# A four-layer attention kernel: the last layer's head moves one iteration ahead, and its exponentials are added up on VectorE alone

## The chip, the cores and the metric

The kernel runs on one core of a Trainium2 chip. The metric is the device time of one execution in microseconds (us); the median of three runs is given. The engines are TensorE (PE, its weight loads are PEld), VectorE (DVE), ScalarE (ACT), GpSimd (POOL) and SyncE (SP, which here only issues DMAs). Each works through its own instructions in order and waits on semaphores.

## The reference

Eight batches of 256 channels x 1024 positions go through four layers. Cut to what matters:

```
x: (8, 256, 32, 32)
L0: q, k, v of 32 channels, softmax attention over 1024 positions, projected and added to x;
    then attention from 1024 positions to 128 concepts, projected and added
L1: q, k of 32 channels, v of 256, softmax attention, x + gamma * out
L2: group norm, q, k, v of 256 channels, one head, softmax attention, projection, x + out
L3: group norm, q, k, v of 256 channels in 8 heads of 32:
    scores = q @ k.T / sqrt(sqrt(32)) ; probs = softmax(scores) ; ctx = probs @ v
    out = layer_norm(ctx @ wo.T + bo) + x
```

All is in float32; the scores are built from high and low parts, so that they keep their precision.

## The kernel before

A batch goes through two halves. Its *front* is layers 0 to 2, its *back* is layer 3, the last layer. `batches` (L150) runs them in three parts: first the fronts of batches 0 and 1 side by side ("fronts"), then six iterations, each with the front of batch b + 2 beside the back of batch b ("both"), then the backs of batches 6 and 7 side by side ("backs"). Every half is written as a generator that issues the instructions of one engine and yields after each slot; `merged` (L136) interleaves two generators of one engine by a fixed table, `ORDER` (L75): numbers of slots, in turn from the second and from the first of the two. So the order on each engine is written out, and an instruction that waits holds all behind it on its engine.

The back of a batch, in order:
- *head*: group norm 3 (DVE statistics, two tiny PE matmuls, ACT log and exponential, DVE and ACT write `hb`); queries and keys of the first four heads (four `project` calls, L605, 16 matmuls as the trace counts them), high parts on ACT (L1067), low parts on DVE (L1280); the values of all heads (L616, 32 matmuls) into `vb`; then SP copies high and low parts into stacks with 24 DMAs (`stacks`, L466)
- *round 0* (`u` = 0, four heads): 32 maxima (PE `max_tile`, L621, two matmuls of 512 columns each into two banks; DVE reduces them, L1285), DVE's transpose and four DMAs that bring the maxima into a row of the queries; queries and keys of the other four heads; 16 steps (`steps`), each with four score matmuls (L641), four exponentials (ACT, L1138), and one weighing of the values (L918)
- *round 1*: the same for the other four heads, without a projection
- the output projection, layer norm (L1498, L1502) and the store.

The sum of the exponentials over the keys is made by adding tiles. In each step from the second on in either half of the queries (14 of the 16 steps), DVE adds the first pair of heads (`add_weights`, L1436, the instruction at L1446), POOL the second pair (L555), each 128 x 1024. The exponentials of a step go into one of two buffers, so ACT waits for both additions before it writes a buffer again (L1131). At the end of a half PE sums over the partitions (L930), ACT makes the logarithm and its exponential, DVE multiplies (L1454).

The front's layers follow the same pattern with one head: `layer0`, `layer1`, `layer2` on PE; maxima (L1285), scores, exponentials (L1008), weighing (L755), POOL's additions (L523, L528), PE's sum (L762), normalising (L1334, L1338). The first matmuls of the front (L608 with `xm`) wait for the input, which SP loads into `xm[b % 3]` (L488) once DVE has read the residual of the back three batches earlier.

The back's tiles are `hb`, `part`, `qs`, `ks`, `vb`, `prb`, `accb`; the front of batch 1 uses the same memory, and the back of batch 7 uses the tiles of the fronts. The back of batch 0 waits on DVE for all of batch 1's front (L1425).

Of the kernel before, what the change touches and what calls it, by code (L numbers as in the profile page):

```python
# [22 lines left out]

# [9 lines left out]
B = 8  # L33
# [25 lines left out]
for _name, _n in (("gn_w2", 2), ("gn_b2", 2), ("bq2", 2), ("bk2", 2), ("bo2", 2), ("gn_w3", 2), ("gn_b3", 2),  # L59
# [36 lines left out]
    ("fronts", "ACT"): (  # L96
        0, 4, 4, 14, 1, 2, 1, 2, 1, 1, 9, 1, 3, 1, 5, 4, 5, 12, 2, 2, 4, 1, 2, 1, 1, 2, 1, 2, 2, 3, 8, 3, 2, 1,
        1, 7, 3, 1, 9, 4, 2, 2, 2, 2, 1, 2, 3, 1, 2, 2, 3, 1, 1, 3, 2, 2, 2, 1, 2, 3, 3,),
    ("both", "ACT"): (
        0, 2, 1, 1, 1, 1, 6, 21, 10, 3, 4, 1, 33, 1, 6, 1, 2, 1, 3, 2, 4, 1, 2, 1, 3, 1, 3, 1, 2, 5, 2, 21, 21,  # L100
        1, 6, 1, 2, 1, 8, 2, 2, 1, 6, 1, 8, 1, 4, 1, 2, 1, 4, 3, 4, 3, 2, 1, 5, 1, 1, 1, 4, 1, 3, 3,),
    ("backs", "ACT"): (
        0, 2, 1, 1, 2, 5, 5, 73, 2, 1, 72, 54, 6, 2, 2, 1, 1, 1, 1, 3, 3, 1, 4, 1, 1, 1, 1, 1, 2, 1, 5, 1, 6, 1,
        1, 4, 4, 2, 3, 1, 1, 1, 4, 1, 4, 2, 3, 1, 8, 1, 4, 1, 18,),
    ("fronts", "DVE"): (
        0, 4, 1, 2, 1, 2, 1, 2, 1, 2, 8, 8, 1, 1, 1, 1, 1, 2, 2, 4, 1, 1, 1, 1, 1, 2, 4, 3, 11, 11, 1, 1, 2, 5,
        1, 5, 6, 2, 3, 2, 2, 1, 4, 2, 2, 1, 2, 1, 6, 3, 1, 1, 1, 2, 1, 1, 6, 2, 1, 1, 1, 1, 2, 4, 4,),
    ("both", "DVE"): (
# [3 lines left out]
    ("backs", "DVE"): (  # L112
# [4 lines left out]
    ("fronts", "POOL"): (  # L117
        0, 5, 4, 3, 4, 1, 1, 3, 3, 2, 2, 1, 1, 1, 1,),
    ("both", "POOL"): (
        10, 1, 3, 1, 1, 6, 6, 1, 3, 1, 3, 2, 2, 4,),  # L120
    ("backs", "POOL"): (
        0, 14, 14, 11, 1, 1, 1, 1, 3, 1, 9,),
    ("fronts", "SP"): (
        0,),
    ("both", "SP"): (
        16,),
    ("backs", "SP"): (
        0, 6, 6, 7, 7, 1, 1, 2, 2,),
# [20 lines left out]

def batches(engine, front, back):  # L150

    finish(merged("fronts", engine, front(0), front(1)))
    for b in range(B - 2):
        finish(merged("both", engine, front(b + 2), back(b)))
    finish(merged("backs", engine, back(B - 2), back(B - 1)))
# [31 lines left out]
def attention_layers(nc, x, weights, vectors, small, concepts, constants, out):  # L187
    with ExitStack() as ctx:
# [255 lines left out]
        def _(sp):  # L444
# [9 lines left out]
            def program(o):  # L454
# [48 lines left out]
        def _(pool):  # L503
# [7 lines left out]
            def program(o):  # L511
# [31 lines left out]
                def back(b):  # L543
# [16 lines left out]
                    def nothing(u):  # L560
                        yield from ()
# [994 lines left out]
```

## Time and profile before

| | us |
|---|---|
| median of 3 runs | 3000.66 (2998.16 to 3001.39) |
| the profiled execution | 3000.55 |
| its span, first to last instruction | 2998.4 |
| busy: PE / DVE / ACT / POOL | 2740.4 / 1795.9 / 1209.4 / 897.0 |

The page gives for each engine the time in which it was busy, then the chain of work that ended last, and the costliest groups of instructions with their mean duration. The windows give the same busy times for a stretch between two points of time, with the granted clock of PE (1.00 is 2.4 GHz, 0.5 is 1.2 GHz). The timeline lists an engine's instructions with start, duration, and how long the engine was idle before and what ended that. A busy PE is not a PE at its peak: matmuls overlap, and at the lower clock the same work is busy for longer.

### The profile page before, as it was taken

The numbers are of one execution on the slowest core, as the hardware profiler recorded it, in microseconds if no ns is written. First come the engines' busy times: TensorE is split into PE (matmuls) and PEld (weight loads), VectorE is DVE, ScalarE is ACT, GpSimd is POOL, SyncE is SP. The second block draws the span as 40 slices with busy tenths as digits, with TensorE's granted clock in tenths as the row PEclk, the third lists the DMA queues.
The fourth block names the chain that finished last, engine by engine and source line by source line (L and its number), as shares of the span: only waits on it lengthen the run. The fifth ranks groups of instructions, "written<-read, shape, count | busy, mean of one in ns | idle before, by whom it ended". The sixth has DMA issues, their size and how long they took to land.

```text
span 2998.4 us, 25561 instructions
## 1 busy us (share of the span) xinstructions
PE 2740.4 (91%) x9636; PEld 1415.0 (47%) x9636; DVE 1795.9 (60%) x1749; ACT 1209.4 (40%) x2073; POOL 897.0 (30%) x362
## 2 busy tenths in 40 slices
PE   7999989999899998999889998999989989798887
PEld 4546644455444544445444454444544445443332
DVE  4535057673676647765476654767447583488884
ACT  3332223535344442534426254262532625325455
POOL 0040311614025240333304242061510615115563
PEclk8899988989788998989979898798987989879787
DMA  2000010100201002010010100101020100211100
GB/s 83 1 0 0 1 43 1 43 1 6 65 1 43 1 17 54 1 42 1 28 43 1 42 1 29 42 14 30 1 56 15 40 3 1 64 36 43 43 1 28
DMA packets 29291, 72.08 MB, mean 24 GB/s; under 512 B 10224, under 2 KB 10416, under 8 KB 28912
## 3 DMA queue, kind: packets, MB, share of 16 engines
q1 hardware_dynamic: 29168, 70.45, 9.4%
q8 instruction: 76, 1.25, 0.2%
q14 instruction: 47, 0.39, 0.0%
HBM read 11.40 MB, written 8.39 MB: 7 GB/s over the span
## 4 chain that ended last, share of the span: by engine, by line
PE 71%; DVE 17%; issue 3%; ACT 3%; SPq 2%; DMA 2%; POOL 1%; DVEq 0%; ACTq 0%; POOLq 0%
PE ps L755 13%; PE ps L608 12%; PE ps L641 9%; PE ps L627 9%; PE ps L918 7%; PE ps L840 6%; DVE ba_nmx L1285 5%; PE ps L616 4%; SPq L477 2%; PE ps L697 2%; DVE accb L1446 2%; PE ps L826 2%; DVE fa_nmx L1285 1%; PE ps L930 1%; PE ps L837 1%
## 5 line engine op out<-in xcount | busy, mean ns | idle before, releaser
L1138 ACT ACTIVATE prb<-ps 128x512 f32<-128x512 f32 x896 | 489.1, 598 | 367.7 <-PE ps L641 341.1
L1285 DVE TENSOR_REDUCE ba_nmx<-ps 128x1 f32<-128x1024 f32 x448 | 531.0, 1215 | 77.9 <-PE ps L627 76.2
L555 POOL TENSOR_TENSOR accb<-accb,prb 128x1024 f32<-128x1024 f32 x168 | 440.8, 2624 | 179.0 <-ACT prb L1138 174.8
L627 PE MATMUL ps<-ks,qs 96*128 96x512 f32 x896 | 419.5, 575 | 74.6 <-DVE ba_nmx L1285 69.0
L555 POOL TENSOR_TENSOR accb<-prb 128x1024 f32<-128x1024 f32 x28 | 80.2, 2864 | 1306.8 <-ACT prb L1138 1247.3
L755 PE MATMUL ps<-pr,h 128*128 128x512 f32 x896 | 421.1, 594 | 0.2
L1446 DVE TENSOR_TENSOR accb<-accb,prb 128x1024 f32<-128x1024 f32 x168 | 317.8, 1892 | 155.8 <-ACT prb L1138 154.1
L641 PE MATMUL ps<-qs,ks 97*128 97x512 f32 x896 | 351.6, 464 | 8.6 <-ACT prb L1138 7.5
L627 PEld LDWEIGHTS ps<-ks,qs 96*128 96x128 f32 x896 | 195.3, 248 | 268.6 <-DVE ba_nmx L1285 201.9
L641 PEld LDWEIGHTS ps<-qs,ks 97*128 97x128 f32 x896 | 160.7, 192 | 228.1 <-ACT prb L1138 157.0
L1008 ACT ACTIVATE pr<-ps 128x512 f32<-128x512 f32 x336 | 194.5, 598 | 175.9 <-PE ps L641 112.5
L755 PEld LDWEIGHTS ps<-pr,h 128*128 128x128 f32 x896 | 167.4, 189 | 162.8 <-issue 143.4
L918 PE MATMUL ps<-prb,vb 128*32 128x512 f32 x1792 | 243.4, 616 | 0.7 <-ACT prb L1138 0.7
L1334 DVE TENSOR_TENSOR tmp<-tmp,rden 128x512 f32<-128x512 f32 x56 | 46.7, 866 | 311.9 <-ACT rden L1020 311.9
L1285 DVE TENSOR_REDUCE fa_nmx<-ps 128x1 f32<-128x1024 f32 x168 | 198.9, 1216 | 17.9 <-PE ps L826 12.2
L523 POOL TENSOR_TENSOR acc<-acc,pr 128x1024 f32<-128x1024 f32 x56 | 153.0, 2732 | 138.8 <-ACT pr L1008 138.8
L608 PE MATMUL ps<-hb,w 128*128 128x512 f32 x368 | 175.8, 632 | 2.0 <-ACT hb L1060 2.0
L840 PE MATMUL ps<-q2k 128*128 128x512 f32 x672 | 173.4, 393 | 0.0
L523 POOL TENSOR_TENSOR acc<-pr 128x1024 f32<-128x1024 f32 x28 | 69.1, 2467 | 338.8 <-ACT pr L1008 301.8
L840 PEld LDWEIGHTS ps<-q2k 128*128 128x128 f32 x672 | 126.7, 189 | 36.4 <-issue 10.3
L608 PE MATMUL ps<-h,w 128*128 128x512 f32 x272 | 139.1, 649 | 1.3 <-DVE bb_nmx L1285 1.3
L627 PE MATMUL ps<-ks,q2k 96*128 96x512 f32 x224 | 90.5, 509 | 36.2 <-DVE fa_nmx L1285 24.6
(303 smaller groups left out, 3402.4 us busy)
## 6 DMA issues: line engine op xcount, KB each, us to landing
qs<-part SPq DMA_DIRECT2D x168, 128.0 KB, 2.4
ks<-part SPq DMA_DIRECT2D x168, 128.0 KB, 2.4
xm<-in_x SPq DMA_DIRECT2D x8, 1024.0 KB, 5.6
out<-prb SPq DMA_DIRECT2D x28, 256.0 KB, 2.0
q2k<-part SPq DMA_DIRECT2D x48, 128.0 KB, 2.4
w<-in_weights SPq DMA_DIRECT2D x1, 2592.0 KB, 8.7
out<-pr SPq DMA_DIRECT2D x4, 256.0 KB, 2.0
qs<-ba_nmx_r SPq DMA_DIRECT2D x56, 4.0 KB, 1.8
```

Of the source, the lines that this page charges most:

```text
L523: pool.tensor_tensor(o.acc[:], before if jg == 1 else o.acc[:], now, ALU.add).then_inc(o.summed[n].sem, 1)
L555: pool.tensor_tensor(o.sums[1], o.pairs[(s - 1) % 2][1] if j == 1 else o.sums[1], o.pairs[s % 2][1], ALU.add)\
L608: mm = pe.matmul(o.ps[0:m, bank, :], wcol(name, kt, m0, m), src[:, kt, cols(ic)], start=kt == 0, stop=kt == CH - 1)
L627: mm = pe.matmul(o.ps[:, bank + jc, :], queries[0:STACK, tile(it)], keys[0:STACK, cols(jc)], start=True, stop=True)
L641: return pe.matmul(o.ps[:, bank, :], keys[0:ROW + 1, tile(jt)], queries[0:ROW + 1, cols(ic)], start=True, stop=True)
L755: mm = pe.matmul(o.ps[:, 2 + ch, :], o.v[:, jt, tile(ch)], o.pr[:, t % 4, :], start=jt == 0, stop=jt == NT - 1)
L840: mm = pe.matmul(o.ps[:, bank, :], kpart[:, kt, keys], qpart[:, kt, cols(ic)], start=False, stop=kt == CH - 1 and kpart is o.kl2)
L918: mm = pe.matmul(o.ps[L * g:L * g + L, 2, :], o.vb[:, jt, L * (QUAD * u + g):L * (QUAD * u + g + 1)], weights3(o, s, g), start=jt == 0, st ...
L1008: act.activation(o.pr[:, t % 4, :], o.ps[:, bank, :], ACT.Exp).then_inc(o.exped[n].sem, 1)
L1138: act.activation(weights3(o, s, g), o.ps[:, turn3[score_use(s, g) % 3], :], ACT.Exp)\
L1285: dve.tensor_reduce(o.nmx[:, head, it:it + 1], o.ps[:, bank:bank + 2, :], AX.XY, ALU.max, negate=True).then_inc(o.max_sb[n].sem, 1)
L1446: dve.tensor_tensor(o.sums[0], o.pairs[(s - 1) % 2][0] if j == 1 else o.sums[0], o.pairs[s % 2][0], ALU.add)\
```

## The change

Three things. First, `batches` makes all backs beforehand and draws each in two pieces: its slots up to the mark "head" run at the tail of the iteration ahead, chained behind the back that ends there, and the rest in its own iteration. The head of batch 0 comes behind the front of batch 1, and the head of batch 7 stays in the last part. Second, DVE issues both additions of a step, pair 0 and pair 1, and POOL none; the two semaphores of the sums keep their meaning. Third, all fifteen tables of `ORDER` are new. The core of the diff (of the tables one stands for all):

```diff
     ("both", "POOL"): (
-        10, 1, 3, 1, 1, 6, 6, 1, 3, 1, 3, 2, 2, 4,),
+        0, 6, 1, 10,),
...
+def head(last_layer):
+
+    for slot in last_layer:
+        yield
+        if slot == "head":
+            return
...
 def batches(engine, front, back):

-    finish(merged("fronts", engine, front(0), front(1)))
+    last = [back(b) for b in range(B)]
+    finish(merged("fronts", engine, front(0), chain(front(1), head(last[0]))))
     for b in range(B - 2):
-        finish(merged("both", engine, front(b + 2), back(b)))
-    finish(merged("backs", engine, back(B - 2), back(B - 1)))
+        finish(merged("both", engine, front(b + 2), chain(last[b], head(last[b + 1]))))
+    finish(merged("backs", engine, last[B - 2], last[B - 1]))
...
@@ SP, back
                         yield from stacks(b, u)
+                        if u == 0:
+                            yield "head"
                         yield from shift_rows(b, u)
...
@@ POOL, back
-                                pool.wait_ge(o.exped[3].sem, o.exped[3].at(b, QUAD * (STEPS3 * u + s + 1)))
...
-                                pool.tensor_tensor(o.sums[1], o.pairs[(s - 1) % 2][1] if j == 1 else o.sums[1],
-                                                   o.pairs[s % 2][1], ALU.add)\
-                                    .then_inc(o.summed_pool.sem, 1)
...
+                    yield "head"
...
@@ PE, back
                         values("v3", o.hb, 2 * half, half).then_inc(o.v_ps[3].sem, 1)
-                        yield
+                        yield "head" if half else None
...
@@ ACT and DVE, back: after take_values
-                    yield
+                    yield "head"
...
@@ DVE, back
-                    def add_weights(u, s):
+                    def add_weights(u, s, pair):
...
-                            dve.wait_ge(o.exped[3].sem, o.exped[3].at(b, QUAD * (STEPS3 * u + s) + 2))
+                            dve.wait_ge(o.exped[3].sem, o.exped[3].at(b, QUAD * (STEPS3 * u + s) + 2 * pair + 2))
...
+                            dve.tensor_tensor(o.sums[pair], o.pairs[(s - 1) % 2][pair] if j == 1 else o.sums[pair],
+                                              o.pairs[s % 2][pair], ALU.add).then_inc(done.sem, 1)
...
-                            if s % NT:
-                                add_weights(u, s)
-                                yield
+                            for pair in range(2):
+                                if s % NT:
+                                    add_weights(u, s, pair)
+                                    yield
```

Read slot by slot, the new tables of PE put this together in an iteration: layer 0 beside the 32 maxima of round 0, the second queries and keys and steps 0 to 6; layer 1's start beside steps 6 to 15 and its chunks beside the maxima of round 1, of which the last 13 come behind layer 1's last sum; layer 2's projections and maxima beside the 16 steps of round 1, the output projection and the layer norm's sums; and layer 2's chunks beside the head of the next batch, whose last slot on PE stands nine slots of the front from the end. In the tables before, the head lies beside the start of layer 0, steps 0 to 15 of round 0 beside layer 1, the maxima of round 1 beside the end of layer 1, its sum, the group norm and the projections of layer 2, and the steps of round 1 beside layer 2's maxima and chunks.

## Rows read from the trace of the kernel before

**Rows 1.** The page: busy time, share and instructions by engine; the chain that ended last.

```profile
PE 2740.4 (91%) x9636; PEld 1415.0 (47%) x9636; DVE 1795.9 (60%) x1749; ACT 1209.4 (40%) x2073; POOL 897.0 (30%) x362
...
PE 71%; DVE 17%; issue 3%; ACT 3%; SPq 2%; DMA 2%; POOL 1%; DVEq 0%; ACTq 0%; POOLq 0%
```

**Rows 2.** Windows after the last iteration: length, busy (instructions) by engine, PE clock, DMA.

```profile
2577.30:2666.80 89.50, 69.25 (x172) 38.96 (x173) 57.57 (x76) 13.28 (x22) 0.00 (x0) 0.68 0.33 77
2666.80:2998.40 331.60, 280.85 (x1101) 114.94 (x1100) 253.53 (x192) 174.42 (x320) 162.45 (x56) 0.84 0.10 26
```

**Rows 3.** Windows of one iteration, cut in four: the same columns.

```profile
1119.80:1227.00 107.20, 89.28 (x263) 47.79 (x263) 76.27 (x87) 28.67 (x44) 0.00 (x0) 0.79 0.18 44
1227.00:1315.80 88.80, 87.76 (x365) 42.10 (x365) 52.26 (x37) 54.20 (x97) 56.70 (x22) 1.00 0.16 36
1315.80:1343.50 27.70, 20.91 (x43) 10.23 (x42) 26.55 (x37) 3.10 (x6) 0.00 (x0) 0.57 0.00 0
1343.50:1482.00 138.50, 137.23 (x533) 74.48 (x532) 67.56 (x58) 65.13 (x115) 54.21 (x22) 0.99 0.01 4
```

**Rows 4.** PE's timeline: start, us, engine, line, out<-in, form, count, [idle before <-releaser].

```profile
392.81 2.41 PE L608 MATMUL ps<-xm,w 128*128 128x512 f32 x5
...
1126.25 1.19 PE L608 MATMUL ps<-xm,w 128*128 128x512 f32 x1 [6.47 <-DMA xm<-in_x]
...
1319.94 1.22 PE L627 MATMUL ps<-ks,qs 96*128 96x512 f32 x2 [1.60 <-DVE ba_nmx L1285]
...
2576.16 1.10 PE L762 MATMUL ps<-acc,ones 128*128 128x512 f32 x2 [0.41 <-issue]
```

**Rows 5.** DVE's timeline in an opening and after the last iteration: the same columns.

```profile
1123.42 1.29 DVE L1334 TENSOR_TENSOR tmp<-tmp,rden 128x512 f32<-128x512 f32 x2 [2.91 <-ACT rden L1020]
...
1195.64 1.23 DVE L1302 STREAM_TRANSPOSE pr<-ps 64x1024 f32<-64x1024 f32 x1
...
1216.77 0.16 DVE L1470 STREAM_TRANSPOSE ba_nmx_t<-ba_nmx 128x32 f32<-128x32 f32 x1
...
2619.38 1.22 DVE L1285 TENSOR_REDUCE ba_nmx<-ps 128x1 f32<-128x1024 f32 x1
```

**Rows 6.** PE's timeline at full clock: what the stages' matmuls take.

```profile
1148.89 3.62 PE L616 MATMUL ps<-w,hb 128*128 128x256 f32 x16
...
1404.97 1.88 PE L755 MATMUL ps<-pr,h 128*128 128x512 f32 x4
...
1408.30 0.63 PE L641 MATMUL ps<-qs,ks 97*128 97x512 f32 x2
...
1410.58 1.06 PE L918 MATMUL ps<-prb,vb 128*32 128x512 f32 x8
...
1459.91 7.03 PE L608 MATMUL ps<-hb,w 128*128 128x512 f32 x16
```

**Rows 7.** The page's costliest groups: busy, mean ns of one, idle time before and releasers.

```profile
L1138 ACT ACTIVATE prb<-ps 128x512 f32<-128x512 f32 x896 | 489.1, 598 | 367.7 <-PE ps L641 341.1
```

**Rows 8.** L1446, DVE's additions: ns min/median/max; their window in the last two backs.

```profile
L1446 DVE TENSOR_TENSOR accb<-accb,prb x168: 1177/1818/3431, 509.9 to 2912.1; 128x1024 f32<-128x1024 f32 x168
...
2666.80:2998.40 331.60, 108.51 (x56) 0.84 0.10 26
```

**Rows 9.** DVE's timeline, then POOL's, in layer 1 of the same iteration.

```profile
1230.90 1.23 DVE L1446 TENSOR_TENSOR accb<-prb 128x1024 f32<-128x1024 f32 x1 [3.92 <-ACT prb L1138]
...
1256.38 2.27 DVE L1446 TENSOR_TENSOR accb<-accb,prb 128x1024 f32<-128x1024 f32 x1
1258.58 3.47 DVE L1285 TENSOR_REDUCE fa_nmx<-ps 128x1 f32<-128x1024 f32 x3
...
1236.05 2.38 POOL L555 TENSOR_TENSOR accb<-prb 128x1024 f32<-128x1024 f32 x1 [117.47 <-ACT prb L1138]
...
1254.43 6.47 POOL L555 TENSOR_TENSOR accb<-accb,prb 128x1024 f32<-128x1024 f32 x2 [0.19 <-ACT prb L1138]
```

**Rows 10.** SP's timeline: the issues of a back's stacks.

```profile
1145.45 7.50 SPq L477 DMA_DIRECT2D qs<-part  x12
```

More of the change, by code:

```diff
@@ L22 @@
 from contextlib import ExitStack
+from itertools import chain
 import concourse.bass as bass
@@ L76 @@
     ("fronts", "PE"): (
[19 rows of a table removed]
[18 rows of a table added]
     ("fronts", "ACT"): (
-        0, 4, 4, 14, 1, 2, 1, 2, 1, 1, 9, 1, 3, 1, 5, 4, 5, 12, 2, 2, 4, 1, 2, 1, 1, 2, 1, 2, 2, 3, 8, 3, 2, 1,
-        1, 7, 3, 1, 9, 4, 2, 2, 2, 2, 1, 2, 3, 1, 2, 2, 3, 1, 1, 3, 2, 2, 2, 1, 2, 3, 3,),
+        0, 4, 4, 10, 1, 2, 2, 3, 1, 2, 1, 2, 14, 2, 2, 4, 4, 2, 1, 1, 1, 1, 7, 2, 4, 1, 1, 1, 9, 5, 1, 1, 1, 1,
+        2, 1, 1, 3, 1, 1, 2, 3, 4, 12, 13, 2, 1, 1, 1, 1, 4, 4, 2, 4, 1, 6, 1, 5, 8,),
     ("both", "ACT"): (
-        0, 2, 1, 1, 1, 1, 6, 21, 10, 3, 4, 1, 33, 1, 6, 1, 2, 1, 3, 2, 4, 1, 2, 1, 3, 1, 3, 1, 2, 5, 2, 21, 21,
-        1, 6, 1, 2, 1, 8, 2, 2, 1, 6, 1, 8, 1, 4, 1, 2, 1, 4, 3, 4, 3, 2, 1, 5, 1, 1, 1, 4, 1, 3, 3,),
+        0, 23, 10, 1, 4, 1, 15, 2, 1, 1, 4, 1, 37, 1, 1, 5, 1, 1, 1, 19, 2, 1, 7, 1, 2, 2, 2, 1, 1, 1, 12, 1, 2,
+        1, 5, 1, 43, 2, 4, 2, 1, 1, 3, 1, 5, 5, 1, 12,),
     ("backs", "ACT"): (
-        0, 2, 1, 1, 2, 5, 5, 73, 2, 1, 72, 54, 6, 2, 2, 1, 1, 1, 1, 3, 3, 1, 4, 1, 1, 1, 1, 1, 2, 1, 5, 1, 6, 1,
-        1, 4, 4, 2, 3, 1, 1, 1, 4, 1, 4, 2, 3, 1, 8, 1, 4, 1, 18,),
[3 rows of a table added]
     ("fronts", "DVE"): (
-        0, 4, 1, 2, 1, 2, 1, 2, 1, 2, 8, 8, 1, 1, 1, 1, 1, 2, 2, 4, 1, 1, 1, 1, 1, 2, 4, 3, 11, 11, 1, 1, 2, 5,
-        1, 5, 6, 2, 3, 2, 2, 1, 4, 2, 2, 1, 2, 1, 6, 3, 1, 1, 1, 2, 1, 1, 6, 2, 1, 1, 1, 1, 2, 4, 4,),
+        0, 4, 1, 2, 1, 2, 1, 1, 2, 3, 7, 5, 3, 3, 2, 6, 3, 2, 4, 4, 2, 1, 3, 1, 3, 1, 25, 3, 1, 1, 2, 1, 2, 2,
+        2, 10, 1, 3, 1, 3, 1, 1, 1, 2, 2, 1, 3, 11, 4, 1, 3, 2, 2, 1, 1, 4, 16,),
     ("both", "DVE"): (
[3 rows of a table removed]
[3 rows of a table added]
     ("backs", "DVE"): (
[4 rows of a table removed]
[5 rows of a table added]
     ("fronts", "POOL"): (
-        0, 5, 4, 3, 4, 1, 1, 3, 3, 2, 2, 1, 1, 1, 1,),
+        1, 1, 3, 1, 4, 6, 6, 1, 1, 1, 1, 6, 1,),
     ("both", "POOL"): (
-        10, 1, 3, 1, 1, 6, 6, 1, 3, 1, 3, 2, 2, 4,),
+        0, 6, 1, 10,),
     ("backs", "POOL"): (
-        0, 14, 14, 11, 1, 1, 1, 1, 3, 1, 9,),
+        1,),
     ("fronts", "SP"): (
-        0,),
+        7,),
     ("both", "SP"): (
-        16,),
+        17,),
     ("backs", "SP"): (
-        0, 6, 6, 7, 7, 1, 1, 2, 2,),
+        6, 7, 8, 1, 1, 1, 1, 1, 1,),
 }
@@ L340, in back_lane @@
             o.weighed = alone("weighed", CH * STEPS3)
-            o.summed_dve = alone("summed_dve", (NT - 1) * IC * CH)[3]
-            o.summed_pool = alone("summed_pool", (NT - 1) * IC * CH)[3]
+            o.summed3 = [alone(f"summed{pair}", (NT - 1) * IC * CH)[3] for pair in range(2)]
             o.total, o.logged, o.inverse, o.taken, o.normed = (
@@ L543, in back @@
                 def back(b):
-                    def steps(u):
-                        for s in range(STEPS3):
-                            ic, j = divmod(s, NT)
-                            if j:
-                                n = IC * u + ic
-                                pool.wait_ge(o.exped[3].sem, o.exped[3].at(b, QUAD * (STEPS3 * u + s + 1)))
-                                if j == 1 and n:
-                                    pool.wait_ge(o.total[3].sem, o.total[3].at(b, n))
-                                if j > 1:
-                                    pool.wait_ge(o.summed_pool.sem, o.summed_pool.at(b, (NT - 1) * n + j - 1))
-                                pool.tensor_tensor(o.sums[1], o.pairs[(s - 1) % 2][1] if j == 1 else o.sums[1],
-                                                   o.pairs[s % 2][1], ALU.add)\
-                                    .then_inc(o.summed_pool.sem, 1)
-                                yield
-                    def nothing(u):
-                        yield from ()
-                    yield from both_rounds(nothing, nothing, steps)
+                    yield "head"
                 return front, back
@@ L925, in sum_weights @@
                             n = IC * u + ic
-                            pe.wait_ge(o.summed_dve.sem, o.summed_dve.at(b, (NT - 1) * (n + 1)))
-                            pe.wait_ge(o.summed_pool.sem, o.summed_pool.at(b, (NT - 1) * (n + 1)))
+                            for done in o.summed3:
+                                pe.wait_ge(done.sem, done.at(b, (NT - 1) * (n + 1)))
                             bank = take_turn(total_use(ic))
@@ L1133, in exps3 @@
                                 used = (NT - 1) * chunk + max(j, 1)
-                                sig = (o.summed_dve, o.summed_pool)[pair]
-                                act.wait_ge(sig.sem, sig.at(b, used))
+                                act.wait_ge(o.summed3[pair].sem, o.summed3[pair].at(b, used))
                             if n == g == 0 and o.before(b) is not None:
@@ L1440, in add_weights @@
                         if j:
-                            dve.wait_ge(o.exped[3].sem, o.exped[3].at(b, QUAD * (STEPS3 * u + s) + 2))
+                            dve.wait_ge(o.exped[3].sem, o.exped[3].at(b, QUAD * (STEPS3 * u + s) + 2 * pair + 2))
                             if j == 1 and n:
                                 dve.wait_ge(o.total[3].sem, o.total[3].at(b, n))
+                            done = o.summed3[pair]
                             if j > 1:
-                                dve.wait_ge(o.summed_dve.sem, o.summed_dve.at(b, (NT - 1) * n + j - 1))
-                            dve.tensor_tensor(o.sums[0], o.pairs[(s - 1) % 2][0] if j == 1 else o.sums[0],
-                                              o.pairs[s % 2][0], ALU.add)\
-                                .then_inc(o.summed_dve.sem, 1)
+                                dve.wait_ge(done.sem, done.at(b, (NT - 1) * n + j - 1))
+                            dve.tensor_tensor(o.sums[pair], o.pairs[(s - 1) % 2][pair] if j == 1 else o.sums[pair],
+                                              o.pairs[s % 2][pair], ALU.add).then_inc(done.sem, 1)
                     def normalise(u, ic):
@@ L1461, in back @@
                     take_values(b, 3, 1, o.vb, 2)
-                    yield
+                    yield "head"
                     def maxima(u):
```

1 line of the change is left out of this document (removed), and 51 rows, old and new, of the table ORDER.

## The prediction

> **What bounds the kernel now.** I read the page's busy times first: TensorE (PE) is busy 91% of the span, VectorE (DVE) 60%, ScalarE (ACT) 40%, GpSimd (POOL) 30% [rows 1]. The chain of waits that ended last runs 71% over PE, 17% over DVE and 1% over POOL [rows 1]. So what can be won is PE's idle time and PE's slow time, and the question is in which stage they lie. PE's timeline gives the stages: the first iteration's layer 0 starts at 392.8 us, the last iteration's last sum ends at 2577.3 [rows 4], so 393 us for the two opening fronts, six iterations of 364.1 on average, and 421 us for the last two back halves, which the windows cut in two [rows 2]. I cut one iteration, the one that begins at 1119.8 us, where PE sums up the front's last weights, into four [rows 3]:
> - opening, 107.2 us: the front's layer 0 beside the back's head, its first 32 maxima and the second queries and keys; PE busy 89.3 us at clock 0.79
> - layer 1, 88.8 us: PE busy 87.8 us at clock 1.00
> - group norm of layer 2, 27.7 us: PE busy 20.9 us at 0.57, DVE busy 26.6 us
> - layer 2, 138.5 us: PE busy 137.2 us at 0.99
>
> The second and fourth are PE at work all the time, the first and third lose. What ends the waits there stands in PE's timeline: after the weights' sum PE is idle 6.47 us until the input of the next front has landed, which is loaded only when the back has read its residual; in the maxima it waits for DVE's reductions, 1.60 us before the pair at 1319.94 [rows 4]. Three reductions in a row take 3.47 us and a single one 1.21, so they start 1.13 us apart [rows 9], while two score matmuls take 0.63 us at full clock [rows 6] (0.56 where more follow, by my estimate): a stretch of maxima alone is bound by DVE.
>
> What PE has to do, at full clock, from PE's timeline [rows 6]: 16 projection matmuls 7.0 us, 32 value matmuls 7.2 us, four weighing matmuls of the front 1.88 us (16 times that, with 16 scores: about 35 us for layer 1's chunks). One step of the last layer is four score matmuls (2 x 0.63) and one weighing (1.06), 2.3 us; for ACT four exponentials of 0.598 [rows 7], 2.4 us.
>
> **Part 1: POOL's additions go to DVE.** 28 additions per batch (7 per round and query half) leave POOL and come to DVE, 224 in all. Those DVE has already take 1.82 us in the median, 1.18 at least and 3.43 at most [rows 8]. The timeline shows when: with POOL idle 1.23 us, beside a POOL addition 2.27 us, and POOL's own go from 2.38 to 6.47 for two [rows 9]. With POOL empty I take 1.2 us for each, the value of DVE alone: 56 x 1.2 = 67 us per batch instead of 28 x 1.8 = 51 us, so DVE gets 16 us more per batch; the bounds are +15 (all at 1.18) and +141 us (all 56 at 3.43). In one iteration DVE goes from 223 (the sum of its four stages [rows 3]) to some 239 of 362 us, on average well under PE. POOL's front sums stay; in the new order they lie mostly beside maxima and single steps.
>
> Locally it is tight. A step asks DVE for 2.4 us, as much as ACT, and PE for 2.3. Where front maxima are mixed in (8 in layer 1, 8 in layer 2) DVE has 10 steps x 2.4 + 8 x 1.13 + 5 of other work = 38 us in layer 1 against PE's 40, and 27.5 against 27 in layer 2. I charge 3 us in layer 1 and 2 us in layer 2. If an addition waits for the step's fourth exponential, what is queued behind it on DVE (maxima) waits too, and PE behind those.
>
> **Part 2: the head one iteration ahead.** The head is group norm 3, the first queries and keys (16 matmuls), the values (32) and 24 DMAs on SP. Per iteration PE's work is the same; its partners are not. Counting slots of the order tables (each number is a run of slots of one half in turn) gives the new company:
> - *Opening.* DVE no longer waits for the head. PE begins with two maxima that need nothing but the stacks, while ACT inverts and DVE normalises (now from the sum at 1119.8 to DVE's normalising at 1123.4 to 1124.7 [rows 5]); the input has long landed, as its load is issued before the head. So layer 0 starts at about +4 us instead of +6.5. 40 maxima x 1.13, the two low parts and copies (4 us) on DVE: 49 us, with the normalising before them the back's maxima are done at +57 (now their transpose is at 1216.8, +97 [rows 5]). PE has 42 us of work there (40 maxima 23, projection 3.5, 16 scores 5, 8 weighings 8.5, shift 2) and fits in. Then layer 0's tail, a chain of transposes and small matmuls, now from the transpose at 1195.6 [rows 5] to 1227.0, 31 us, with six steps (14 us of PE) and the second queries and keys (7 us) to fill it: 28 us. Opening: 85 instead of 107.2 us, with six steps more and the head less in it.
> - *Layer 1*: from its projection to its first score 3.5 + 7.2 + 5 + 10 steps x 2.3 + 1 + the 3 us = 43 us; then 35 us of its chunks with 18 back maxima (10 us of PE): 45. 88 instead of 88.8.
> - *Group norm of layer 2*: 13 maxima (14.7), normalising (2.8), statistics (3.1), then the small steps to the first projection (5): 26 instead of 27.7.
> - *Layer 2*: 138.5, minus 8 maxima (4.5) that are done by then, plus the head (14.3), plus 2 us for DVE and 2 for the chain of the back's end: 152.
>
> The sum is 351: 11 us under the iteration cut here (362.2), 13 under the average of 364.1. I take 13. Six iterations: -78 us.
>
> *Where the head isn't hidden.* For batch 0 it stands behind both fronts on every engine, as DVE waits for the second front, whose tiles it overwrites. Its chain alone is in the trace at the start of the last two backs: from the sum at 2577.3 to the first maximum 2619.4, 42 us [rows 4, 5], with 15 us of it SP issuing 24 DMAs of 0.62 us [rows 10]. Layer 0 of the next front is queued behind two such maxima on PE, and starts now right after the sum, at 392.8 [rows 4]; less the 6 us that the other openings lose anyway: +36 us. Bounds: +14 (the work alone) and +42.
>
> *The last two backs.* Now 89.5 us pass from the sum (2577.3) to the end of the first back's 32 maxima (2666.8). After: normalising 6, 32 maxima 36, the other back's statistics and low parts on DVE 6, 2 of stalls: 50. -39 us. The other back's head runs beside, and its maxima begin at the same place as now. The 331.6 us after that have now DVE busy 253.5, PE 280.9 at 0.84, POOL 162 [rows 2]; DVE has 109 us of additions in it [rows 8]; after, 112 x 1.2 = 134, and POOL's coupling is gone: 0, bounds -30 and +25.
>
> The tables of the two opening fronts are new as well; nothing in their slots but the head speaks for a gain or a loss: 0, bounds -10 and +10. Everything else (renamed semaphores, "head" markers) costs nothing: no instruction is behind it. The profiled run is 3000.55 us (span 2998.4 and 2.1 around it), as good as the median 3000.66. Sum: 3000.55 - 78 + 36 - 39 + 0 = 2919.5, predicted 2918 us.
>
> **A rule that speaks against it.** In stretches where PE only feeds maxima its granted clock is 0.57 to 0.79 [rows 3], that is, partly its lower level of 1.2 GHz. The Trainium skill ("TensorE: Matmul & The Clock Gate", Part 1) says that the slow level is the default and that only activity releases it. By the rule a new opening paced by DVE's maxima would stay slow all through; this is the rival "slow opening" below.
>
> **The rivals.**
> - *More than forecast.* The maxima in the last backs no longer interleave with a POOL that holds every step (POOL is busy 162 us there, in 56 additions), so the 331.6 us fall by 30, and the stages of layers 1 and 2 lose none of my 5 us: -30 - 30 = 2858 us. For it: 49% of POOL in that stretch; against it: DVE and PE are each near full there too.
> - *Slow opening.* Over the 57 us of maxima PE has 42 us of work at full clock; at a mean clock of 0.63, between the 0.57 and 0.79 of [rows 3], 67 us: +10 us per iteration, 2918 + 60 = 2978 us. For it: those clocks; against it: layer 0 makes PE far busier there than 13 maxima do in the norm stage.
> - *DVE becomes the bound, slower than before.* DVE does its queue in order, and now has both pairs' additions, each waiting for its own exponentials, between the maxima PE waits for. If each of the 224 moved additions costs the path 0.63 us beyond my charge, 141 us come back: 3059 us. It decides from 0.37 us per addition on (82 / 224). For it: DVE busy 26.6 of 27.7 us in the norm stage, and the balance of 2.4 to 2.3 us; against it: 40% of DVE is idle, and POOL's 2.4 to 3.2 us per step were no faster.
> - *It doesn't do what it says*: the head still ends last, since SP needs 15 us for its DMAs and the next maxima wait for them. But some 15 us of layer 2's chunks follow the head's last slot on PE. No price of its own beyond the slow opening's.
>
> **How the numbers follow.** Forecast (2890 to 2950 us) 0.49; more than forecast 0.20; slow opening or a DMA that isn't hidden 0.14; about no change 0.04; slower 0.13. About 0.2% (6 us) is what a measurement of this kernel can tell from nothing. Faster 0.83, same 0.04, slower 0.13. The range leaves out the slower rival and the far end of the gain: 2850 to 2978.
>
> **What would show it.** Right: no PE idle for the input at the iteration's start; L1446 at about 1.2 us on 448 instructions, POOL with only the front's 128 left; iterations of 351 us; a gap of about 40 us without layer 0 after the opening fronts; the first 32 maxima of the last backs done 50 us after the last sum. Wrong: L1446 far over 1.3 us, PE's waits for DVE's maxima grown by more than the waits for input and norms shrank, iterations above 358 us.

## The result, and the profile after

The changed kernel takes 2926.86 us (2925.09 to 2932.88, 4 runs) against 2999.64 us for the kernel before beside it: a ratio of 0.9761, 95% interval 0.9744 to 0.9778. The forecast was 2918 us. The profiled execution took 2927.05 us with a span of 2924.9, so it can stand for the median. The change moves the line numbers by a few: DVE's additions are at L1439 (L1446 before), the exponentials at L1130, the maxima at L1277, the projections at L601, the sums of the last layer over the partitions at L923.

First the page: busy time by engine, the chain that ended last, and the rows of the exponentials and the additions (answer to [rows 1, 7, 8]).

```profile
PE 2673.6 (91%) x9636; PEld 1380.7 (47%) x9636; DVE 1857.2 (63%) x1973; ACT 1210.1 (41%) x2073; POOL 270.2 (9%) x138
...
PE 74%; DVE 18%; ACT 4%; issue 2%; SPq 1%; DMA 0%; DVEq 0%; ACTq 0%
...
L1130 ACT ACTIVATE prb<-ps 128x512 f32<-128x512 f32 x896 | 483.5, 601 | 319.4 <-PE ps L634 279.4
...
L1439 DVE TENSOR_TENSOR accb<-accb,prb 128x1024 f32<-128x1024 f32 x336 | 394.0, 1217 | 14.8 <-ACT prb L1130 14.2
```

POOL lost its 224 instructions and DVE got them, yet DVE is busy only 61 us longer: each addition takes 1.217 us on the mean where it took 1.89 (1.82 in the median). PE does the same 9636 matmuls in 67 us less of busy time, at a better clock.

Next one iteration, from the front's last sum at 1140.1 us to the next at 1491.7, cut at the same four places as [rows 3], with the same columns:

```profile
1140.10:1231.60 91.50, 80.29 (x274) 38.87 (x273) 73.67 (x73) 32.68 (x54) 0.00 (x0) 0.87 0.00 1
1231.60:1317.30 85.70, 84.19 (x331) 42.85 (x330) 66.66 (x60) 43.62 (x75) 16.70 (x8) 1.00 0.17 37
1317.30:1341.60 24.30, 14.11 (x30) 6.23 (x29) 22.34 (x34) 2.94 (x5) 0.00 (x0) 0.62 0.00 1
1341.60:1491.70 150.10, 148.96 (x569) 81.83 (x570) 67.98 (x79) 72.08 (x126) 16.79 (x8) 0.98 0.14 36
```

The opening is 15.7 us shorter and its clock rose from 0.79 to 0.87; layer 2 has taken in the head and is 11.6 us longer. In sum 351.6 us.

PE's timeline and then SP's where the first batch's head stands bare, and PE's at the start of an iteration (answer to [rows 4, 10]):

```profile
434.68 2.05 PE L620 MATMUL ps<-ks,qs 96*128 96x512 f32 x4 [8.12 <-DMA ks<-part]
436.53 1.91 PE L601 MATMUL ps<-xm,w 128*128 128x512 f32 x2
...
417.60 7.57 SPq L487 DMA_DIRECT2D qs<-part  x12
425.21 7.57 SPq L487 DMA_DIRECT2D ks<-part  x12
...
1142.91 2.41 PE L601 MATMUL ps<-xm,w 128*128 128x512 f32 x5 [1.89 <-DVE tmp L1326]
```

In the iterations the wait for the input (6.47 us before) is gone; 1.89 us for DVE's normalising stand in its place. But after the opening fronts layer 0 starts only at 436.5 us, behind the head's 24 DMAs of 0.63 us and its first two maxima.

Last, the windows of that gap and of the last two backs (answer to [rows 2]):

```profile
399.60:436.50 36.90, 19.84 (x56) 12.60 (x57) 10.85 (x22) 6.83 (x11) 0.00 (x0) 0.71 0.38 86
2546.40:2601.80 55.40, 45.04 (x119) 25.51 (x117) 47.49 (x55) 6.90 (x11) 0.00 (x0) 0.74 0.26 58
2601.80:2924.90 323.10, 272.71 (x1103) 114.80 (x1102) 261.19 (x249) 173.33 (x320) 0.00 (x0) 0.86 0.11 27
```

The ledger, from the profiled executions (the stretches are cut at the front's last sums, as in the prediction; the iterations are averages, so the changes add up to -73.7):

| stretch | before | after | change | forecast |
|---|---|---|---|---|
| opening fronts | 392.7 | 399.6 | +6.9 | 0 |
| head of batch 0, bare (389.1 - 351.5) | | 37.6 | +37.6 | +36 |
| six iterations | 364.1 each | 351.5 each | -75.6 | -78 |
| last two backs, to the 32nd maximum | 89.5 | 55.4 | -34.1 | -39 |
| the rest of them | 331.6 | 323.1 | -8.5 | 0 |
| sum | 2998.4 | 2924.9 | -73.5 | -81 |

### The profile page after: what moved, and what is told of

Its sections match the earlier page's. It is cut to its first block, busy times and chain, and to the rows that moved or that the text cites. A ratio compares the mean times of both kernels' runs of the same rounds, so it can differ in the third digit from the quotient of the medians.

```text
span 2924.9 us, 25567 instructions
## 1 busy us (share of the span) xinstructions
PE 2673.6 (91%) x9636; PEld 1380.7 (47%) x9636; DVE 1857.2 (63%) x1973; ACT 1210.1 (41%) x2073; POOL 270.2 (9%) x138
## 4 chain that ended last, share of the span: by engine, by line
PE 74%; DVE 18%; ACT 4%; issue 2%; SPq 1%; DMA 0%; DVEq 0%; ACTq 0%
PE ps L748 15%; PE ps L601 12%; PE ps L634 11%; PE ps L911 7%; PE ps L620 7%; DVE ba_nmx L1277 6%; PE ps L833 6%; PE ps L609 5%; DVE fa_nmx L1277 3%; PE ps L690 2%; PE ps L819 2%; ACT prb L1130 2%; DVE bb_nmx L1277 1%; DVE accb L1439 1%; PE ps L830 1%
## 5 line engine op out<-in xcount | busy, mean ns | idle before, releaser
L1130 ACT ACTIVATE prb<-ps 128x512 f32<-128x512 f32 x896 | 483.5, 601 | 319.4 <-PE ps L634 279.4
L1277 DVE TENSOR_REDUCE ba_nmx<-ps 128x1 f32<-128x1024 f32 x448 | 529.9, 1216 | 96.8 <-PE ps L620 94.4
L620 PE MATMUL ps<-ks,qs 96*128 96x512 f32 x896 | 374.6, 524 | 84.4 <-DVE ba_nmx L1277 64.1
L748 PE MATMUL ps<-pr,h 128*128 128x512 f32 x896 | 421.3, 595 | 1.6 <-ACT tmp L1029 1.0
L1439 DVE TENSOR_TENSOR accb<-accb,prb 128x1024 f32<-128x1024 f32 x336 | 394.0, 1217 | 14.8 <-ACT prb L1130 14.2
L620 PEld LDWEIGHTS ps<-ks,qs 96*128 96x128 f32 x896 | 182.3, 227 | 266.3 <-DVE ba_nmx L1277 185.6
L748 PEld LDWEIGHTS ps<-pr,h 128*128 128x128 f32 x896 | 168.8, 190 | 148.6 <-issue 134.7
L1277 DVE TENSOR_REDUCE fa_nmx<-ps 128x1 f32<-128x1024 f32 x168 | 199.8, 1216 | 43.6 <-PE ps L819 37.6
L601 PE MATMUL ps<-hb,w 128*128 128x512 f32 x368 | 179.2, 634 | 13.5 <-DVE ba_nmx L1277 9.2
L535 POOL TENSOR_TENSOR acc<-acc,pr 128x1024 f32<-128x1024 f32 x56 | 132.6, 2369 | 237.7 <-ACT pr L1001 237.7
L601 PE MATMUL ps<-h,w 128*128 128x512 f32 x272 | 139.1, 644 | 14.7 <-ACT h L1053 14.7
L601 PEld LDWEIGHTS ps<-hb,w 128*128 128x128 f32 x368 | 73.4, 203 | 104.8 <-issue 85.3
L634 PE MATMUL ps<-q2k,ks 97*128 97x512 f32 x224 | 119.7, 561 | 1.0 <-ACT pr L1001 0.8
L620 PE MATMUL ps<-ks,q2k 96*128 96x512 f32 x224 | 99.0, 539 | 22.7 <-DVE ks L1266 11.9
```

Of the source, the lines that this page charges most:

```text
L535: pool.tensor_tensor(o.acc[:], before if jg == 1 else o.acc[:], now, ALU.add).then_inc(o.summed[n].sem, 1)
L601: mm = pe.matmul(o.ps[0:m, bank, :], wcol(name, kt, m0, m), src[:, kt, cols(ic)], start=kt == 0, stop=kt == CH - 1)
L620: mm = pe.matmul(o.ps[:, bank + jc, :], queries[0:STACK, tile(it)], keys[0:STACK, cols(jc)], start=True, stop=True)
L634: return pe.matmul(o.ps[:, bank, :], keys[0:ROW + 1, tile(jt)], queries[0:ROW + 1, cols(ic)], start=True, stop=True)
L748: mm = pe.matmul(o.ps[:, 2 + ch, :], o.v[:, jt, tile(ch)], o.pr[:, t % 4, :], start=jt == 0, stop=jt == NT - 1)
L1130: act.activation(weights3(o, s, g), o.ps[:, turn3[score_use(s, g) % 3], :], ACT.Exp)\
```

## The experiments

Each kernel ran beside the kernel before. The iteration lengths below are means over iterations 2 to 6, read from PE's timeline between the ends of the front's last weighing matmuls (L755 before, L748 after). The same mark ends the opening fronts and starts the last two backs, so these figures stand about 1 us off the ledger's.

### One part alone

**The order alone.** All new tables and the head ahead, but POOL adds up the second pair again, its slots in ACT's order:

```diff
 # DVE, step
+                                    if pair == 0:
                                         add_weights(u, s, pair)
 # POOL, back
+                                pool.wait_ge(o.exped[3].sem, o.exped[3].at(b, QUAD * (STEPS3 * u + s + 1)))
+                                pool.tensor_tensor(o.sums[1], o.pairs[(s - 1) % 2][1] if j == 1 else o.sums[1],
+                                                   o.pairs[s % 2][1], ALU.add).then_inc(done.sem, 1)
```

> The changed kernel with its new order, but the second pair's additions are back on POOL, in an order that follows ScalarE's. Theory A (the gain is the order: the head beside layer 2, no wait for the input, maxima and steps in other company): about 2940 us, with iterations of 352 to 355 us; VectorE's additions go back to about 1.8 us, and the last two backs are some 9 us longer. Rival B (the gain is POOL's absence, which took VectorE's port): most of it is lost, about 2985 us, iterations near 362.

Measured: 3026.21 us, 1.0087 of before (1.0072 to 1.0102). Neither theory held: the whole gain is lost and more, and the new order without the other part is slower than the kernel before.

**The additions alone.** Old tables and head, DVE adds both pairs in the six iterations, in the slot of its own addition. In the old order of the last two backs the engines would then wait for each other, so POOL keeps its additions there.

```diff
 # DVE, step
                                 add_weights(u, s)
+                                add_second(u, s)   # pair 1, if b < B - 2
```

> The kernel before with its old order; in the six iterations VectorE makes both pairs' additions (the second pair's of a step stands ahead of the first pair's of the next step), in the last two backs POOL keeps its own, as the old order there does not allow the move. Theory A (TensorE bounds the stages with additions): iterations of 362 to 367 us, 3000 to 3015 us in all. Rival B (freedom from POOL is the gain): iterations of 355 to 358, 2955 to 2965 us. Rival C (VectorE becomes the bound in the old order): 3040 us or more.

Measured: 3036.13 us, 1.0122 (1.0104 to 1.0139). Slower too, between theory A (3015 at most) and theory C (3040 at least).

So two parts that cost 26 and 36 us each alone win 73 us together. (Neither kernel had its tables fitted anew as a whole: the order alone takes those of the change, with new ones for POOL only, and the additions alone keeps the old ones. What a full fit would give either is not shown.) Windows of one iteration each, of the kernel before, the additions alone, the order alone and after show where (columns as above):

```profile
1480.50:1845.30 364.80, 337.93 (x1201) 175.62 (x1200) 222.99 (x217) 151.16 (x259) 110.94 (x45) 0.89 0.10 24
```
```profile
1499.90:1872.00 372.10, 341.41 (x1201) 175.69 (x1200) 241.62 (x245) 151.29 (x259) 37.53 (x17) 0.89 0.10 23
```
```profile
1167.30:1532.50 365.20, 332.57 (x1201) 171.05 (x1200) 225.53 (x216) 151.22 (x259) 111.18 (x44) 0.92 0.10 24
```
```profile
1139.30:1490.90 351.60, 327.55 (x1201) 169.78 (x1200) 230.65 (x244) 151.32 (x260) 33.50 (x16) 0.93 0.10 25
```

The order takes the clock from 0.89 to 0.92 or 0.93 in both its forms. The rest is PE's idle time (length less busy): 26.9, 30.7, 32.6 and 24.1 us.

*What holds the order alone* stands in the steps between two groups of maxima. Windows of the same work, after and the order alone, then POOL's, DVE's and PE's timeline of the order alone at the end of that stretch:

```profile
1200.40:1275.60 75.20, 73.29 (x327) 33.84 (x328) 59.55 (x59) 47.06 (x81) 0.00 (x0) 0.98 0.04 10
```
```profile
1229.70:1310.30 80.60, 73.23 (x327) 33.37 (x328) 56.67 (x46) 47.13 (x81) 39.32 (x14) 0.98 0.10 22
```
```profile
1297.95 9.83 POOL L567 TENSOR_TENSOR accb<-accb,prb 128x1024 f32<-128x1024 f32 x3
...
1301.06 4.52 DVE L1456 TENSOR_TENSOR accb<-accb,prb 128x1024 f32<-128x1024 f32 x2
...
1307.88 1.94 PE L940 MATMUL ps<-accb,ones 128*32 128x512 f32 x8 [3.73 <-issue]
```

POOL's last three additions take 3.28 us each and end at 1307.78; PE's sum over the partitions, which needs them, starts at 1307.88 after 3.73 us idle. The row gives "issue" because it names no releaser; the times name it. PE's waits for that sum are 7.1 us in this iteration against 0.8 in after, those for ACT's exponentials, which wait for POOL's and DVE's additions to free a buffer, 4.8 against 1.9. DVE, rid of half its additions, is busy 56.7 us instead of 59.6: nearly as long, since beside POOL each one takes longer.

*What holds the additions alone* is DVE's queue in the old order. Windows of one stretch of steps, before and with the additions alone:

```profile
1578.00:1634.50 56.50, 55.48 (x240) 26.40 (x239) 39.91 (x36) 35.07 (x60) 24.23 (x9) 0.99 0.01 1
```
```profile
1597.10:1657.20 60.10, 56.35 (x239) 26.05 (x238) 43.77 (x45) 35.06 (x60) 0.00 (x0) 0.99 0.00 1
```

and the group of that stretch that waits most on PE (busy, mean ns | idle before, releaser), with the additions alone:

```profile
L629 PE MATMUL ps<-ks,q2k 96*128 96x512 f32 x16 | 5.4, 427 | 2.0 <-DVE fa_nmx L1287 2.0
```

Before, PE was busy 55.5 of 56.5 us there: no wait to win. With nine instructions more on DVE, PE waits 3.75 us instead of 1.0, 2.0 of it for the front's maxima that are queued behind them.

### Are the additions themselves the price, on either engine?

In four kernels the additions of the second pair from the third key tile on (j > 1: 192 of 224, which is 168 of 196 without batch 7, whose tiles have other names; 144 of 168 in the six iterations) are cut to one column, waits and queue as they were. These leave out most of the second pair's sums.

```diff
+    narrow = slice(0, IW if j == 1 else 1)
-    tensor_tensor(o.sums[1], ..., o.pairs[s % 2][1], ALU.add)
+    tensor_tensor(o.sums[1][:, :, narrow], ..., o.pairs[s % 2][1][:, :, narrow], ALU.add)
```

**New order, DVE (the whole change), cut.**

> The changed kernel, where the second pair's additions from the second on in each half are one column wide instead of 512, some 0.15 us instead of 1.22 (196 of them, so 205 us of VectorE's work are left out; the sums of the second pair are incomplete). It prices VectorE's additions on the path. Theory A (tight in two places per iteration, 5 us, and in the last backs): iterations of 346 to 348 us, 2885 to 2900 us in all. Rival (VectorE is off the path altogether): 2920 to 2927 us. Rival (VectorE is the bound): 2800 us or less.

Measured: 2924.89 us (2919.22 to 2931.13), 0.9749 (0.973 to 0.9769): 2 us less than uncut, which is within the spread of its runs. DVE's busy time fell by 188 us, to 1669.1, and nothing came back. The rival expectation holds.

**New order, POOL (the order alone), cut.**

> The run with the order alone (new order, additions of the second pair on POOL) with POOL's additions at j>1 cut to one column wide: 168 of its 196 additions in the last layer leave out all but one column of each head's sums. Order alone took 3026.2 us, the whole change 2926.9, so 99 us stand between them. Theory A: they are POOL's additions themselves, their 2.80 us each and what DVE's own additions lose beside them (mean 2.13 us there, 1.22 with POOL idle): then this takes 2915 to 2940 us and DVE's additions fall to about 1.3 us. Theory B: they are the places of POOL's queue in the order, whose waits stay as they are: then it stays above 2990 us.

Measured: 2937.07 us, 0.9787 (0.9762 to 0.9812), 89 us less than uncut, DVE's additions at 1.27 us on the mean. Theory A.

**Old order, DVE (the additions alone), cut.**

> The run with the additions alone (old order, DVE adds for both pairs in the six iterations, 3036.1 us) with the added additions at j>1 cut to one column wide, which leaves out the rest of the second pair's sums; the waits and the queue are the same. Theory A: it was 35 us slower than before because 1.22 us of DVE stand ahead of the fronts' work in each step (a steps stage there went from 56.5 to 60.1 us with PE idle 1.0 to 3.75): then it falls to 2985 to 3005 us. Theory B: the wait for the second pair's exponentials at each addition, one place too early in DVE's queue, is the loss: then it stays above 3020 us.

Measured: 2995.09 us, 0.9982 (0.9972 to 0.9993), 41 us less than uncut. Theory A.

**Old order, POOL (the kernel before), cut.**

> The kernel before with POOL's additions at j>1 in the last layer cut to one column wide, which leaves out the rest of the second pair's sums; order and waits as before. Theory A: in the old order PE sets the steps stages (busy 55.5 of 56.5 us and 34.0 of 34.6), so that nothing is won by taking POOL's work and DVE's delay away there, and only the last two backs gain: 2975 to 2998 us. Theory B: POOL's additions hold the old order too, as they do the new one: below 2960 us.

Measured: 2958.25 us, 0.9855 (0.9826 to 0.9883): by the number theory B. The trace divides it: the iterations don't change, which is theory A, and the last two backs fall by 35 us, far more than A had for them.

Together, one iteration and the last two backs in us:

| | old order: iteration | last two backs | new order: iteration | last two backs |
|---|---|---|---|---|
| POOL adds the second pair | 364.5 | 422.7 | 365.2 | 394.4 |
| the same, cut | 364.4 | 387.4 | 355.0 | 367.5 |
| DVE adds it | 372.1 | (POOL) 415.5 | 351.5 | 379.4 |
| the same, cut | 365.2 | (POOL) 415.5 | 353.0 | 370.7 |

Each order fits one engine. In the old one POOL's additions cost the iterations nothing and DVE's 7 us each; in the new one DVE's cost nothing and POOL's 10. With the additions out of the way the order is worth 9 to 12 us per iteration. The order is where the gain comes from, and the move of the additions is what lets it through. (That the last two backs of the kernels with DVE's additions in the old iterations take 415.5 instead of 422.7, with the same instructions in them, was not looked into.)

### Contention, or waiting for POOL?

**POOL beside, nobody waits.** The whole change, and POOL adds on a tile of its own at the places it has in the order alone (each of the three additions waits for the one before):

```diff
+    pool.wait_ge(o.exped[3].sem, o.exped[3].at(b, QUAD * (STEPS3 * u + s + 1)))
+    for _ in range(3):
+        pool.tensor_tensor(scratch[:], scratch[:], scratch[:], ALU.add)   # 128 x 320
```

> The whole change, DVE adds for both pairs; and POOL, at the 196 places where it added in the run with the order alone, runs three additions of 320 columns on a tile of its own that nobody reads or waits for. Its output is complete. Apart from the fronts' few additions behind them in POOL's queue, only the two engines' work beside one another is new. Theory A, working beside each other is the price: DVE's 392 additions go from 1.22 to about 1.9 us or more, some 270 us of DVE's time, and the kernel takes 2990 to 3060 us. Theory B, the price was that ACT and PE waited for POOL's 2.8 us chain, and DVE has room for its own delay: it takes 2927 to 2945 us.

Measured: 3068.71 us, 1.0228 (1.0203 to 1.0252), iterations 368.6. The lines of DVE's and POOL's additions (ns: least, median, most), and one iteration:

```profile
L1457 DVE TENSOR_TENSOR accb<-accb,prb x336: 1207/1734/1747, 517.2 to 3024.2; 128x1024 f32<-128x1024 f32 x168
...
L567 POOL TENSOR_TENSOR scratch<-scratch x672: 717/1516/1759, 516.1 to 3052.4; 128x320 f32<-128x320 f32 x168
```
```profile
1176.10:1544.70 368.60, 334.70 (x1201) 171.06 (x1200) 249.17 (x244) 151.64 (x260) 134.10 (x100) 0.91 0.10 23
```

Theory A for the time; its 1.9 us per addition was too high (1.54 on the mean of the 336). DVE is busy 18.5 us longer in an iteration and the iteration is 17 longer. The dose is not that of the order alone: three pieces came to 3.6 us, against 2.80 for POOL's one addition there. And the fronts' few additions are queued behind the new ones on POOL, which this run can't keep apart.

**POOL's addition in four pieces.** The order alone, each addition cut into four of 256 columns:

```diff
+    for k in range(4):
+        piece = slice(IW // 2 * (k % 2), IW // 2 * (k % 2 + 1))
+        add = pool.tensor_tensor(o.sums[1][:, k // 2, piece], old[:, k // 2, piece],
+                                 o.pairs[s % 2][1][:, k // 2, piece], ALU.add)
```

> The run with the order alone (3026.2 us) with each of POOL's additions in the last layer cut into four of 256 columns, one after the other, the same columns in all. What is asked is how DVE and POOL stand in each other's way: wholly beside POOL, DVE's additions took 3.21 us at the median (3.41 at most) against 1.22 alone, where POOL's were 1024 columns (2.34 us alone), and 1.74 us at the median (1.75 at most) where POOL's were 320 columns (0.72 us alone). Theory A, each waits out a whole instruction of the other: DVE's longest fall to about 1.7 us, and POOL's pieces, some 0.6 us alone, take up to 1.8. Theory B, they share by columns while both run: DVE's median wholly beside POOL stays near 3 us. The kernel's time by A: POOL's addition becomes up to 7 us where DVE is busy without a break, 2.4 where it isn't: 3000 to 3060 us; by B 3025 to 3040 us.

Measured: 3100.19 us, 1.0338 (1.0319 to 1.0357), iterations 375.1. The same lines for the order alone (one addition of 1024 columns) and for the four pieces:

```profile
L1456 DVE TENSOR_TENSOR accb<-accb,prb x168: 1208/2261/3410, 515.0 to 2981.2; 128x1024 f32<-128x1024 f32 x168
...
L567 POOL TENSOR_TENSOR accb<-accb,prb x168: 2344/2840/3380, 517.7 to 2980.7; 128x1024 f32<-128x1024 f32 x168
```
```profile
L1460 DVE TENSOR_TENSOR accb<-accb,prb x168: 1209/1526/1817, 512.6 to 3043.4; 128x1024 f32<-128x1024 f32 x168
...
L570 POOL TENSOR_TENSOR accb<-accb,prb x672: 717/730/1809, 516.7 to 3055.8; 128x256 f32<-128x256 f32 x168
```

DVE's longest in these rows fell from 3.41 to 1.82 us as theory A has it, so as a rule an addition waits out one instruction of the other engine. One of batch 7's, which has another row, does not fit that: it took 5.07 us while six of POOL's pieces ran beside it one after another. The time is above A's 3060: POOL's pieces take 0.72 us at least where I had put 0.6, so its addition grew from 2.80 to 3.65 us, and the kernel got 74 us slower although DVE lost less. Together with the run before: DVE's delay alone is enough to lose the gain, and the length of POOL's chain costs by itself. How the 14 us per iteration of the order alone divide between the two stays open.

### What the change left on the table

**Batch 0's head inside the first iteration.** Its slots are taken out of the opening tables, and the first iteration gets tables of its own in which batch 0's head stands at the start:

```diff
-    finish(merged("fronts", engine, front(0), chain(front(1), head(last[0]))))
+    finish(merged("fronts", engine, front(0), front(1)))
     for b in range(B - 2):
-        finish(merged("both", engine, front(b + 2), chain(last[b], head(last[b + 1]))))
+        finish(merged("both" if b else "first", engine, front(b + 2), chain(last[b], head(last[b + 1]))))
```

> The changed kernel, but the head of batch 0 runs inside the first iteration, beside layer 0 as in the order of before, with a table of its own for that iteration. Theory A (the 37 us of the exposed head are its chain and its DMAs, which layer 0 can cover in part): the part from the opening fronts' last sum to the end of the first iteration falls from 389 to about 373 us, 2911 us in all. Rival (the head's work of 14 us and the waits for VectorE's maxima come in anyway): 385 us, 2923 us in all.

Measured: 2915.33 us, 0.9716 (0.9699 to 0.9732), 11.5 less than the whole change. The first iteration falls from 389.1 to 374.4 us: theory A.

**The old order of the opening fronts**, with batch 0's head behind them as a block (only the "fronts" tables differ):

> The whole change, but the order of the opening fronts is the old one, with the first batch's head behind it as a block. The opening stretch took 392.7 us before and 399.6 after. Theory A: the 6.9 us are the new order of the fronts themselves and come back in full: 2920 us. Theory B: they are time that the head's pieces take and that it would take at the end as well: 2927 us.

Measured: 2917.38 us, 0.9727 (0.9714 to 0.9741). The opening, to the last weighing, takes 390.4 us instead of 398.7, like the 387.2 to 391.9 of the four kernels with the old order (there the last weighing is the other front's). Theory A, and 2.6 us better than it said. The head's pieces are not what made it slow: the kernel with the head inside the first iteration has the new order without them, and its opening takes 403.0.

**Both.** The "first" tables and the old fronts:

> The first batch's head inside the first iteration (2915.3 us in its run) together with the old order of the opening fronts. Theory A: both gains add up: 2908 us. Theory B: the opening was slow by the head's pieces, which are not there any more in the run with 2915.3: the old order of the fronts gives nothing on top, 2915 us.

Measured: 2907.39 us (2906.81 to 2910.27), 0.9694 (0.9681 to 0.9707). The two gains of 11.5 and 9.5 us nearly add up, theory A, and this is the fastest kernel here: 19.5 us under the change as made.

## Why the prediction was right, and where it wasn't

- *Iterations.* Forecast 351 us, found 351.5, at the cut places 91.5 / 85.7 / 24.3 / 150.1 against 85 / 88 / 26 / 152. The opening is 6.5 us longer than I had it, the other three are 5.9 shorter. The opening in four windows (columns as above; the maxima end at 1200.4), and two rows of PE's timeline behind them:

```profile
1140.10:1160.00 19.90, 13.37 (x40) 6.93 (x39) 17.46 (x18) 5.47 (x7) 0.00 (x0) 0.82 0.00 1
1160.00:1171.00 11.00, 9.01 (x24) 6.07 (x24) 9.07 (x10) 1.02 (x1) 0.00 (x0) 0.50 0.00 0
...
1200.40:1212.00 11.60, 11.55 (x35) 5.95 (x35) 6.58 (x10) 3.03 (x5) 0.00 (x0) 0.85 0.01 1
1212.00:1231.60 19.60, 19.15 (x83) 7.41 (x83) 13.85 (x15) 12.96 (x24) 0.00 (x0) 1.00 0.00 0
...
1200.45 8.83 PE L601 MATMUL ps<-hb,w 128*128 128x512 f32 x16 [1.52 <-DVE ba_nmx L1277]
1225.76 3.70 PE L730 MATMUL ps<-acc,wo_con 64*128 64x512 f32 x8
```

  The maxima are done at +60.3 instead of +57. I had PE's work there at full clock, and the clock was 0.82 and then 0.50 in the first 31 us; how much of the 3.3 us that is stays open. The tail after them takes 31.2 instead of 28, and here a term was missing: I took it for a chain with 21 us of PE's work beside it (14 of steps, 7 of the projection), but PE is busy 30.7 of the 31.2 us. The projection takes 8.83, and layer 0's own matmuls of the tail, which I had not counted, some 8.8 (3.70 of them in the last row).
- *The stated 5 us per iteration for a tight DVE* (3 in layer 1, 2 in layer 2) was no cost: with the additions cut to a column the iteration is not shorter (353.0 against 351.5). The two stages came out at 85.7 and 150.1, which is my sum without the charge. That the total still fits is luck: the 6.5 us that I had too few in the opening took its place. The rival "DVE becomes the bound" fell with the same run; the run with POOL beside shows how near it is, as 18.5 us more of DVE's time came through almost whole.
- *Additions at 1.2 us.* 1.217 on the mean, 1.227 at most. Right, for the reason given: with POOL empty DVE takes 1.2.
- *Slow opening.* Over the whole opening the clock rose from 0.79 to 0.87 rather than fall, with PE busy 80.3 of 91.5 us. The rival was there in part all the same: in the 11 us at 0.50 PE is at its lower level throughout, after 20 us in which it had been busy 13.4. The norm stage, maxima with little beside them, stayed low at 0.62 (0.57 before). So it looks like a matter of company, as I had it against the rival; no run varied the company alone.
- *Bare head.* +37.6 against +36, with bounds 14 and 42. The run with the head inside shows that 11.5 us of it were a choice of place.
- *Last two backs.* The maxima -34.1 against -39, the rest -8.5 against 0. Larger costs hide behind these sums: with POOL's additions cut the old order loses 35 us over the last two backs, so the rival "more than forecast" had found a true cost. Of the 43.3 us by which the two backs fell in all (422.7 to 379.4) the order alone gives 28.3 and DVE in place of POOL 15.0, and DVE's second additions still cost 8.7 there (379.4 against 370.7).
- *Opening fronts: the step that failed.* I took 0 with bounds of 10 either way, since nothing in the slots spoke for a loss; the new fronts tables cost 6.9 us in the ledger and 9.5 when undone. What in them costs it was not found. The error stayed within my bounds. Against the sum of -81 the stretches are off by +6.9, +1.6, +2.4, +4.9 and -8.5 us, 7.3 together, and that the largest of them is of the other sign is luck. (The sum gives 2919.5; the 2918 that I put down has no term for its last 1.5 us.)
- *What the prediction never asked* is whether its parts add up. I priced the head and the additions one by one, and my first two expectations rested on it: 2940 to 2985 for the order alone and 2955 to 3015 for the additions alone, where 3026 and 3036 came. The forecast for both was near because each stage was summed with both in place.

## What to carry to other kernels

Where engines run by a written order, the order is fitted to the durations and owners of the work in it. Judge a move of work and the order that goes with it as one thing, and don't price either by a run of the other alone. Cutting the moved work to one column, waits kept, tells in one run whether its owner has room for it: 2 us for DVE in the new order, 89 for POOL. And where a piece of work is shifted by one turn of a loop, look at its first turn, which no other turn hides: here a table of its own for the first iteration gave 11.5 us.

## What the runs showed of the hardware

Two additions on DVE and POOL, both with all operands in SBUF, don't share; one waits. I sorted each kernel's 128 x 1024 additions on DVE from 400 us on by how much of them lies beside a POOL instruction. With POOL idle they take 1.22 us. Those that lie beside POOL for at least 95% of their time:

| POOL's instruction | alone | DVE's addition, median | most | POOL's own, most |
|---|---|---|---|---|
| 1024 columns, the kernel before | 2.34 | 1.34 | 3.43 | 3.46 |
| 1024 columns, the order alone | 2.34 | 3.21 | 3.41 | 3.44 |
| 320 columns | 0.72 | 1.74 | 1.75 | 1.76 |
| 256 columns | 0.72 | 1.56 | 1.81 | 1.81 |

The median differs between two orders with the same instructions (1.34 and 3.21), as either engine can be the one that waits. The most goes with the length of the other's instruction, with the one exception of 5.07 us told above, where DVE's addition started at 3025.83 and POOL's pieces ran without a break to 3029.82.

DVE's maxima, which read PSUM and write one column, don't notice: 73 of them lay wholly beside POOL's instructions in the order alone and took 1.212 us on the mean, as against 1.217. This agrees with the Trainium skill ("SBUF — State Buffer", Who interferes with whom): DVE and GpSimd contend through the one pair of ports that they share and nowhere else, and it is held exclusively; a `tensor_tensor` with both inputs in SBUF contends with GpSimd's reads, and `tensor_reduce` never contends on trn2.

Moving half of DVE's additions to POOL relieved DVE of next to nothing: in the new order it is busy 1834.8 us with POOL's help and 1857.2 without, 22 us for 224 additions of 1.22 us, 273 us in all. And short instructions on POOL cost more per column: 1024 columns take 2.34 us at the least, 256 and 320 columns both 0.72, and two columns, alone, 0.20. So four pieces of 256 take 2.9 us instead of 2.34 even when nothing stands in their way.
